# Attention outputs turned to head order by DMA transposes of f16 parts in place of TensorE transposes

## The reference

```python
q = rmsnorm(rope((h @ Wq_c @ Wq_up)), q_norm_w)            # 16 heads x 128
c_out  = softmax([q @ ck.T * scale | sink]) @ ck           # 64 compressed keys, one for 16 tokens
sw_out = softmax([50*tanh(q @ k_sw.T*scale/50) | sink]) @ v_sw   # window of 64 tokens
ao = (c_out + sw_out)                                       # b, t, 16 heads, 128
inter = einsum('btgf,gfi->btgi', ao.reshape(b, t, 4, 512), Wg)
x = layernorm(x + inter.reshape(b, t, 1024) @ Wo)
x = layernorm(x + x @ ternary(weight).T + bias)
```

## Time and profile before

| | before |
|---|---|
| median of 3 executions | 470.46 us (470.4 to 470.9) |
| profiled execution | 468.88 us, its span 466.9 us |
| mean granted TensorE clock | 0.979 |
| PE busy | 416.7 us (89%) |
| DVE busy | 352.2 us (75%) |
| ACT busy | 271.5 us (58%) |
| POOL busy | 213.2 us (46%) |
| transfers | 33.43 MB, 64 transposes from the SP queue |

### The profile page before, as it was taken

How to read it: one execution, slowest core, us unless ns; L and a number is a source line. 1 busy time by engine, 2 the same in 40 slices (tenths; PEclk the granted TensorE clock), 3 DMA queues, 4 the chain that set the end, 5 groups by cost and what they waited for, 6 DMA issues and landing times.

```text
span 466.9 us, 8984 instructions
## 1 busy us (share of the span) xinstructions
PE 416.7 (89%) x3374; PEld 355.7 (76%) x3376; DVE 352.2 (75%) x660; ACT 271.5 (58%) x784; POOL 213.2 (46%) x142
## 2 busy tenths in 40 slices
PE   3899979959988989999999999989898999998982
PEld 2795858757967888887878887869696889787881
DVE  1144889777889889898888888889898988973421
ACT  2131453775675859595848484847667685847300
POOL 0000402060655656464746563736556565654504
PEclk9999999978999999999999999999999999999995
DMA  8990000838314040605060505042431514060000
GB/s 225 317 297 0 2 1 1 225 85 231 64 30 86 18 90 14 96 8 101 1 103 2 103 1 101 13 92 35 69 68 37 66 38 91 14 91 13 0 13 22
DMA packets 80652, 33.43 MB, mean 72 GB/s; under 512 B 68961, under 2 KB 79201, under 8 KB 80353
## 3 DMA queue, kind: packets, MB, share of 16 engines
q1 hardware_dynamic: 78640, 30.98, 30.6%
q10 hardware_dynamic: 1968, 1.88, 1.6%
HBM read 11.87 MB, written 4.19 MB: 34 GB/s over the span
## 4 chain that ended last, share of the span: by engine, by line
PE 56%; DVE 15%; ACT 12%; issue 9%; DMA 3%; POOL 2%; SPq 1%; POOLq 0%; DVEq 0%; ACTq 0%
PE PS L552 10%; PE PS L498 8%; PE PS L573 8%; ACT room_h L716 7%; PE PS L464 5%; PE PS L512 4%; DVE room_wg L977 4%; PE PS L531 3%; PE PS L600 3%; PE PS L478 3%; PE PS L375 3%; PE PS L428 3%; DMA H<-in_L_attn_h 3%; DVE room_K L992 2%; PE PS L363 2%
## 5 line engine op out<-in xcount | busy, mean ns | idle before, releaser
L552 PE MATMUL PS<-Weff,aoT 128*128 128x256 f32 x768 | 98.0, 283 | 0.0
L552 PEld LDWEIGHTS PS<-Weff,aoT 128*128 128x128 f32 x768 | 92.4, 188 | 0.1
L1062 POOL TENSOR_TENSOR ny<-nx,nu 128x16 f32<-128x16 f32 x16 | 46.7, 2921 | 96.5 <-DVE nx L904 96.5
L1056 POOL TENSOR_TENSOR room_wg<-room_comp,keep 128x1024 f32<-128x1024 f32 x32 | 75.9, 2396 | 6.2 <-ACT room_comp L707 6.2
L573 PE MATMUL PS<-V,room_wg 128*128 128x129 f32 x512 | 68.1, 286 | 7.0 <-POOL room_wg L1056 2.7
L573 PEld LDWEIGHTS PS<-V,room_wg 128*128 128x128 f32 x512 | 64.3, 198 | 10.6 <-ACT room_h L716 3.6
L716 ACT ACTIVATE room_h<-PS,room_K 128x8 f32<-128x8 f32 (+7 forms) x256 | 70.6, 365 | 1.8 <-DVE room_K L931 1.7
L716 ACT ACTIVATION_READ_ACCUMULATOR room_h<-PS,room_K 128x1 f32 x256 | 62.3, 249 | 0.0
L632 ACT ACTIVATE room_wo<-PS 128x128 f32<-128x128 f32 (+7 forms) x16 | 10.4, 652 | 76.1 <-PE PS L591 76.1
L984 DVE TENSOR_TENSOR aoT<-PS,aoT 128x1024 fp32r<-128x1024 f32 x32 | 38.9, 1224 | 16.6 <-ACT aoT L632 16.3
L498 PE MATMUL PS<-room_h,kT 128*128 128x512 f16 x192 | 46.5, 379 | 2.3 <-DVE aoT L984 1.4
(11 more groups left out here) (143 smaller groups left out, 723.2 us busy)
## 6 DMA issues: line engine op xcount, KB each, us to landing
H<-in_L_attn_h SPq DMA_DIRECT2D x4, 512.0 KB, 8.9
room_wg<-in_L_attn_Wg SPq DMA_DIRECT2D x1, 2048.0 KB, 12.5
cw_rows<-room_wgT SPq DMA_DIRECT2D x1, 2048.0 KB, 6.8
CW<-cw_rows SPq DMA_DIRECT2D x1, 2048.0 KB, 8.3
out<-room_wo SPq DMA_DIRECT2D x16, 128.0 KB, 1.7
CW<-in_L_attn_Wq_up ACTq DMA_DIRECT2D x2, 512.0 KB, 9.0
room_wo<-in_L_attn_Wo SPq DMA_DIRECT2D x1, 1024.0 KB, 14.9
room_h<-room_K SPq DMA_TRANSPOSE x64, 3.3
```

The lines of the kernel that those rows point to most:

```text
L552: last = nc.tensor.matmul(o, aoT[:, ap, hd // 2, hd % 2, :, :].rearrange("p c q -> p (c q)"), Weff[:, wp, hd, :], start=mid and hd == n == ...
L1056: G.tensor_tensor(Pm[:, c, :, :], E[:, c, :, :], keep[:, :, :], ALU.mult).then_inc(g_mask, 1)
L1062: G.tensor_tensor(ny[:, 0:HEADS], nx[:, 0:HEADS], nu[:, 0:HEADS], ALU.pow).then_inc(g_rs, 1)
```

## The change

`ao` is no longer turned by PE. ACT writes its f16 high part from SBUF to `ao16[:, 0]` (`output_high`), POOL the f16 low part to `ao16[:, 1]` (`output_low`, a subtraction), and SP issues four more DMA transposes in each step (`outputs`): each takes 64 partitions x 2048 f16, where those of the queries take 128 x 1024. The projection has three products a head as before, now with f16 operands on both sides, and is split otherwise: all 32 products with the high part first, the 16 with the low part after `values(0)`. So that the f16 parts hold the range, V, the ones' column and `e1` are scaled by a power of two, `Weff` by another, both worked out in the setup from maxima of |V|, |Wg| and |Wo|; the result is scaled back in the addition of H. PSUM banks 2 and 3 take the transposes of the compressed probabilities.

```diff
# SP
+            def outputs(i):
+                wait(sp, p_o, i)
+                for n, ready in ((0, a_at), (1, g_al)):
+                    sp.wait_ge(ready, 2 * i + 2)
+                    for r in range(2):
+                        sp.dma_start(aoT[:, n, r, :, :].rearrange("p a (c q) -> p (a c) q", q=WIN),
+                                     ao16[r * WIN:(r + 1) * WIN, n, :, :, :].rearrange("p a c d -> p (a c d)"),
+                                     transpose=True).then_inc(s_ah if n == 0 else s_al, 16)
+                if i >= 2:
+                    store(i)
...
+                if 0 <= i < NT:
+                    outputs(i)
# PE, setup, between the transposes of Wg and the queries of tile 0
+            pe.wait_ge(s_big, 1)
+            b = begin(G_MT)
+            end(nc.tensor.transpose(b[0:3, 0:P], big[:, :], ident[:, :]))
+            pe.wait_ge(s_diag, 1)
+            b = begin(G_MB)
+            end(nc.tensor.matmul(b[:, 0:3], ones[0:3, :], big_d[:, :], start=True, stop=True))
# PE, queries; feed-forward; window scores
-                        wait(pe, *((d_al, 2 * t - 3) if hf else (a_ct, t - 1)))
+                        wait(pe, d_ql, 2 * t + hf - 1)
+                        if hf:
+                            wait(pe, a_ct, t - 1)
...
+                    if not mid:
+                        pe.wait_ge(d_ao, 2 * NT)
...
-                        wait(pe, *((d_ao, 2 * i), (d_al, 2 * i), (d_al, 2 * i), (a_tanh, 4 * i + 1))[u])
+                        wait(pe, *((a_tanh, 4 * i + 1) if u == 3 else (d_ao, 2 * i)))
# PE, projection (the low part follows values(0))
-                    pe.wait_ge(a_at, 2 * t + 2)
-                    pe.wait_ge(d_al, 2 * t + 2)
...
+                    pe.wait_ge(s_ah, 32 * t + 32)
+                def project_high():
+                    for hd in range(HEADS):
+                        for wp in range(2):
+                            last = nc.tensor.matmul(o, aoT[:, 0, hd % 2, hd // 2, :], Weff[:, wp, hd, :],
+                                                    start=mid and hd == wp == 0, stop=False)
+                    return last
+                def project_low():
+                    pe.wait_ge(s_al, 32 * t + 32)
+                    for hd in range(HEADS):
+                        last = nc.tensor.matmul(o, aoT[:, 1, hd % 2, hd // 2, :], Weff[:, 0, hd, :],
+                                                start=False, stop=not mid and hd == HEADS - 1)
# PE, end of the step
-                def output_T(c):
-                    pe.wait_ge(d_ao, 2 * i + c + 1)
-                    for pr in range(PAIRS):
-                        last = nc.tensor.transpose(bank((2, 4)[c], 2)[:, pr * P:(pr + 1) * P], ao[:, c, pr, :], ident[:, :])
-                    last.then_inc(p_at, 1)
# ACT: output_high(0), then the compressed probabilities, then output_high(1)
+                    def output_high(c):
+                        act.wait_ge(d_ao, 2 * i + c + 1)
+                        wait(act, s_ah, 32 * i)
+                        narrow(ao16[:, 0, :, c, :], ao[:, c, :, :], a_at)
# DVE, setup, between the copies of e1 and the sink's parts
+            for n, data in enumerate((V[...], wg_s[:, :, :], wo_s[:, :, :])):     # 2048, 4096, 2048 elements
+                last = V_.tensor_reduce(big[:, n:n + 1], data, AX.XY, ALU.max, apply_absolute_value=True)
+            last.then_inc(s_big, 1)
...
+            V_.tensor_scalar(V[:, :, D], V[:, :, D], v_inv, None, ALU.mult).then_inc(s_unit, 1)
# DVE, step
-                def output_rest(c):
-                    dve.wait_ge(a_at, 2 * i + c + 1)
-                    V_.tensor_tensor(aoT[:, 1, :, :, c, :], bank((2, 4)[c], 2)..., aoT[:, 0, :, :, c, :], ALU.subtract)
# POOL: output_low(0) after the product with the compressed sums, output_low(1) after x1b
+                def output_low(c):
+                    pool.wait_ge(a_at, 2 * i + c + 1)
+                    wait(pool, s_al, 32 * i)
+                    G.tensor_tensor(ao16[:, 1, :, c, :], ao[:, c, :, :], ao16[:, 0, :, c, :], ALU.subtract).then_inc(g_al, 1)
```

More of the change, by code:

```diff
@@ L15 @@
 NT = BATCH * SEQ // P
-EARLY = 12
 SPREAD = 2.0 ** 3.5
@@ L76, in build @@
         ckTs = sb("ckTs", [P, 2, BATCH * NBLK], f16)
-        ckTv = sb("ckTv", [P, 2, BATCH * NBLK], f32r)
-        Weff = sb("Weff", [P, 2, HEADS, HID], f32r)
+        ckTv = sb("ckTv", [P, 2, BATCH * NBLK], f16)
+        Weff = sb("Weff", [P, 2, HEADS, HID], f16)
         CW = sb("CW", [P, CHUNKS, HID])
@@ L102, in build @@
         K = room_K[:, :].rearrange("p (t d) -> p t d", d=D)
+        big, big_t, big_d = sb("big", [P, 3]), sb("big_t", [3, 1]), sb("big_d", [3, 3])
+        bound, unit = sb("bound", [P, 3]), sb("unit", [P, 4])
+        v_unit, w_unit, v_inv, w_inv = (unit[:, n:n + 1] for n in range(4))
+        o_inv = sb("o_inv", [P, 1])
         fsum, fscale, fthr, fthn = (sb(n, [P, 1]) for n in ("fsum", "fscale", "fthr", "fthn"))
@@ L164, in build @@
         s_fs, s_fw = sem("s_fs"), sem("s_fw")
+        s_big, s_diag, s_unit = sem("s_big"), sem("s_diag"), sem("s_unit")
         s_sm, s_e, s_keep = sem("s_sm"), sem("s_e"), sem("s_keep")
@@ L214, in build @@
         NAMES = ("H", 8), ("K", 4), ("CR", 1), ("CK", 1), ("XC", 4), ("V", 4), ("FS", 1), ("KT", 4), ("CKT", 1), \
-            ("WG", 8), ("WE", 8), ("CW", 8), ("FT", 1)
+            ("WG", 8), ("MT", 1), ("MB", 1), ("WE", 8), ("CW", 8), ("FT", 1)
         starts = dict(zip((n for n, _ in NAMES), np.cumsum([0] + [c for _, c in NAMES]).tolist()))
-        G_H, G_K, G_CR, G_CK, G_XC, G_V, G_FS, G_KT, G_CKT, G_WG, G_WE, G_CW, G_FT = starts.values()
-        by_scalar = [g % 2 == 0 if g < G_CW else g - G_CW not in (2, 4, 6) for g in range(G_FT + 1)]
+        G_H, G_K, G_CR, G_CK, G_XC, G_V, G_FS, G_KT, G_CKT, G_WG, G_MT, G_MB, G_WE, G_CW, G_FT = starts.values()
+        by_scalar = [g % 2 == 0 and g not in (G_MT, G_MB) if g < G_CW else g - G_CW not in (2, 4, 6) for g in range(G_FT + 1)]
         def gbank(g):
@@ L544, in step @@
                         project_blocks(True, range(groups(t)))
-                    pe.wait_ge(a_at, 2 * t + 2)
-                    pe.wait_ge(d_al, 2 * t + 2)
[L548 to L554, removed]
+                    pe.wait_ge(s_ah, 32 * t + 32)
[10 more added lines that the diff above has]
+                                                start=False, stop=not mid and hd == HEADS - 1)
                     return last
                 if proj and mid:
-                    project_heads(range(EARLY))
+                    project_high()
                 elif proj:
-                    project_heads(range(HEADS)).then_inc(p_o, 1)
+                    project_high()
+                    project_low().then_inc(p_o, 1)
                 def values(c):
@@ L581, in step @@
                 if proj and mid:
-                    project_heads(range(EARLY, HEADS))
+                    project_low()
                     project_blocks(False, range(groups(t))).then_inc(p_o, 1)
@@ L590, in probs_T @@
                     for g in chunks:
-                        last = nc.tensor.transpose(bank(n)[:, (g % 4) * P:(g % 4 + 1) * P],
+                        last = nc.tensor.transpose(bank(2 + n)[:, (g % 4) * P:(g % 4 + 1) * P],
                                                    Ec[:, SUB * g:SUB * (g + 1), :], ident[:, :])
@@ L680, in output_weights @@
                     act.wait_ge(s_ps, G_WE + g + 1)
-                    nc.scalar.activation(Weff[:, 0, 2 * g:2 * g + 2, :], two(G_WE + g), ACT.Copy).then_inc(s_wh, 1)
+                    if g == 0:
+                        act.wait_ge(s_unit, 1)
+                    nc.scalar.mul(Weff[:, 0, 2 * g:2 * g + 2, :], two(G_WE + g), w_unit).then_inc(s_wh, 1)
             def step(i, front, mid, proj, ffn):
```

84 lines of the change are left out of this document (50 added, 34 removed).

## The result

| | before | after |
|---|---|---|
| median | 469.48 us (20 executions, 466.64 to 470.9) | 472.36 us (20 executions, 470.67 to 475.77) |
| ratio | | 1.0062, 95% interval [1.0044, 1.008] |
| profiled execution | 468.88 us, span 466.9 | 475.77 us, span 474.0 |
| granted clock, mean | 0.979 | 0.943 |

The account below looks back on a forecast made before the run. The prediction took a ring through DVE, ACT and PE to bound the kernel. Setup +15.1, step 1 +1.8, steps -13.3 and tail -0.2 gave +3.4 us on a 470.46 us median: 473.9 us, range 464 to 487.

Parts of the forecast that it names:

- setup: Before PE's L464: maxima and hand-overs delay it by 12.8 us, the lowered clock adds 2.3; together +15.1 us.
- step 1: First output transposes queue behind the CW read, so L552 starts 2.7 us later: +1.8 us, bounds -1 and +4.
- fourteen steps: Shorter way from one end of divide(1) to the next: 0.95 us gained a step, -13.3 us in all.
- tail: After the last divide(1): wait of 0.4 us against 0.6 saved, -0.2 us; +3 if the landing is late.
- POOL: Low part takes 2.4 us on POOL ahead of power and first mask, with 1.4 us free.
- Output transposes: On SP's queue: 1.3 us an issue, 3.3 us to landing, DMA share 0.56.
- Rival D: Output transposes of 64 partitions cost more; at twice issue and transfer 520 us; chance 0.07.
- The Trainium skill's price of the DMA path: At 1309 ns a block the added transposes cost 42 us a step, over 700 us in all; chance 0.01.
- Rival B: Steps gain more, DVE's hand-over being the whole ring: 466 us at 1.5 us a step; chance 0.17.
- ring: Loop through DVE, ACT and PE, from one end of divide(1) to the next: 21.6 us, predicted 20.7.

Follow-up runs that it names:

- e1: Changed kernel with the scaling powers of two as constants, without maxima and small products: 457.59 us, 0.9749 of the kernel before.
- e5: Changed kernel with output transposes over 128 partitions x 1024 in place of 64 x 2048 (output mixed): 470.71 us, 1.001 of the kernel before.
- e2: Changed kernel with the same maxima taken earlier on DVE, where it idled in the setup: 462.19 us, 0.985 of the kernel before.
- e3: Changed kernel with the CW read split, only its first chunk ahead of the first output transposes: 468.97 us, 0.9988 of the kernel before.
- e4: Changed kernel with POOL's low part of the second half tile computed twice a step: 488.05 us, 1.0387 of the kernel before.
- e12: e11 with the squares of half the heads ahead of the high part on ACT: 460.61 us, 0.9824 of the kernel before.
- e6: Changed kernel with the next tile's squares ahead of the second half's high part on ACT: 490.2 us, 1.0425 of the kernel before.
- e10: Changed kernel with the edits of e5 and e6 together: 478.98 us, 1.0231 of the kernel before.
- e13: e12 with unread products on PE where it would idle: 457.45 us, 0.9742 of the kernel before.
- e8: Changed kernel with output transposes by half tile, eight issues of 64 x 1024 in place of four: 485.51 us, 1.0302 of the kernel before.
- e9: Changed kernel with e6 and e8 together and the second low part on DVE: 489.01 us, 1.0391 of the kernel before.
- e11: Changed kernel with e2 and e3 together, the two small products moved behind tile 0's queries: 459.68 us, 0.9808 of the kernel before.

## Why the prediction was right, point by point

The profiled difference by stages: setup to D0 +16.1, step 1 +4.15, fourteen steps -14.3, tail +1.2, together +7.1, the difference of the spans. Seven experiments have the same setup, with D0 from 123.06 to 125.21 and a median of 123.6, so this execution's 125.52 is high by 1.9. Step 3 took 22.28 us in it, as in e1 and e5, but 20.51 in e2 and e3; it isn't in every execution. In the three long ones the queries' last transpose lands 2.0 us after D in place of 0.3 to 0.4, PE waits 1.1 to 1.2 us for it, and the first window scores take 2.1 to 2.7 us in place of 1.46 as the clock falls:

```profile
173.26 2.25 PE L532 MATMUL PS<-room_h,kT 128*128 128x512 f16 x6 [1.22 <-DMA room_h<-room_K]
```

Without both the stages read +14.1, +4.15, -16.1, +1.2 = +3.4, with step 3 as it was +5.1; predicted +15.1, +1.8, -13.3, -0.2 = +3.4, and the medians say +2.9. So the sum is right to 0.5 us by the medians, but part of that is luck: step 1 and the tail are off by 2.4 and 1.4 us one way, the steps by 1.0 to 2.8 the other, and the setup by 1.0 either way. Which of these an execution at the median has isn't shown, as e1's and e5's were close to theirs with a long step 3.

- **Setup: right.** Reductions 8.8 (predicted 8.9), the last ends at 76.85 (76.7), L496 from 78.93 (78.6). The clock was at 0.50 from 76 to 85, and L496 lost 1.7 of the 1.8 expected. The products of Weff lost 1.3 (15.25 us for L458, 13.97 before) in place of 0.5. e1's D0, 0.3 us behind before's, shows that little else is in it.
- **Step 1: mis-sized**, the mechanism right. The transposes landed at 135.9, 4.86 us after PE wanted them. The term had 1.8 with the clock's fall as its upper bound of 4; the fall happened (5.45 us for the 32 products in place of 3.65), and the step grew by 4.15. e3 takes 3.7 us of the step away again, all of it by the earlier start of the products.
- **Steps: mechanism right, for a gain of 0.95 a step the profile has 1.02, and 1.15 with step 3 as in e2.** In the step shown L961 came at D+2.10 (2.3), L512 at 3.24 (3.57), DVE waited 0.34 (0.7) ahead of L990, `divide(0)` began at 13.19 (13.55), the next D at 20.40 (20.7). The 0.3 us lie on ACT: high part, squares and the copy of x1's transposes were over at D+3.19 (3.5), and the feed-forward waited for that copy. Another error cost nothing. The window scores were to begin at D+1.8, on the queries' landing counted from the end of an issue; landing counts from its start, one issue earlier, and x1's last operation on POOL set them off instead, at D+0.74. PE then stood idle for 1.05 us ahead of L512.
- **POOL: right in price, thin in cover.** The low part took 2.12 us (2.4 taken). The forecast saw 1.4 us free; e4 shows 0.8.
- **Output transposes: wrong in price, nearly harmless here.** 1.3 us an issue, 3.3 to landing and a DMA share of 0.56 were expected, 1.85, 4.4 and 0.73 measured. Rival D was right that 64 partitions cost more (e5) and wrong on by how much: 1.4 times the issue, 1.3 times the landing. The second landed at D+6.8 (D+7.2 expected), which is luck: landing takes 1.1 us longer than taken, but was again counted from the issue's end. In other steps it landed up to 1.1 us after PE wanted it, and e5, where these waits are gone, shows that the steps get no shorter.
- **Tail: +1.2 in place of -0.2.** The clock fell to 0.55 (450 to 453 us) behind two waits of 1.11 and 0.86 us, so that the blocks took 5.31 us, 3.62 before. The low part then waits 0.83 us for its transposes at the end, which the term left out. In e2 and e3 the blocks take 3.62 and the tail 25.6 and 25.2 us, against 25.1 before and 26.3 here.

```profile
450.05 5.31 PE L565 MATMUL PS<-CW,room_wo 128*128 128x256 f32 x16
...
459.68 1.92 PE L593 MATMUL PS<-Weff,aoT 128*128 128x256 f16 x16 [0.83 <-DMA aoT<-ao]
```

- **The Trainium skill's price of the DMA path** (VectorE: DVE Perf Modes, "The three transpose paths", 1309 ns a block of 128 x 128) again doesn't hold: 64 blocks a step use 0.73 of 20.5 us of the DMA engines, 15.0 us in all, against an estimate of 84 us by that price.

Rival B's condition, 1.2 us a step, was nearly met, and e12 shows 0.3 to 0.7 more in single steps. What stops it there is a landing that a shorter ring exposes.

## What to carry to other kernels

A constant that is worked out on the chip costs its place in the program more than its work: the same three maxima cost 14.7 us in front of TensorE (e1) and 4.7 where VectorE idled (e2). Shortening a ring exposes what was hidden just beneath it, here a DMA landing that varies between 4.4 and 6.4 us; look how much room each arrival has before moving its consumer forward. And a wait of TensorE of 2 us or more is to be priced with what the clock may take behind it; after other waits a shorter one was enough here.

## What the runs showed of the hardware

- Waits of TensorE ahead of the 32 high products in e6, e10, e12 and e13, step 1 left out: from 2.6 to 2.9 us all three were followed by the lower clock and by 5.1 to 5.3 us for products that else take 3.65; from 1.9 to 2.5 us eight were (4.9 to 5.3 us) and five were not. In e8 and e9 all five waits of 2.6 to 3.9 us were, and two of six from 2.1 to 2.5.
- Shorter waits were enough where others had gone before: three in a row (1.42, 0.84, 1.93 us) in e11's setup, 1.27 us in step 1 of e3, 1.11 and 0.86 in after's tail (not in e2's and e3's, with the same two waits).
- Unread products of 0.9 us ahead of the wait kept the clock up in one step of e13 with a late landing (wait 1.69 us), and not in another (2.26 us).
- A DMA transpose from SBUF costs its queue 1.2 to 1.3 us whether it moves 128 x 1024 or 64 x 1024 f16, and 1.8 to 1.9 for 64 x 2048 behind another; landing, from the issue's start, is 3.3, 2.7 and 4.4 us. What the late landings of up to 6.4 us meet stays open.
- A subtraction of 1024 elements with an f16 operand and result takes POOL 2.13 us, a product of as many in fp32 alone (L1114) 2.35.
